# Another order of work in the single-head stage, in normalised products and around head 11 of a transformer kernel

## The reference, cut to what matters

```python
q = x @ w_q.T; k = ctx @ w_k.T; v = ctx @ w_v.T
x = x + alpha * (softmax(q @ k.T / sqrt(512)) @ v) @ w_o.T      # single-head stage
for i in (1, 2):                                                # two layers
    h = layer_norm(x) * scale_i + offset_i
    qh, kh, vh = heads(h @ wq + bq), heads(ctx @ wk + bk), heads(ctx @ wv + bv)
    kh, vh = append(kh, bias_k), append(vh, bias_v)             # one more key and value
    x = x + (softmax(qh @ kh.T / sqrt(128)) @ vh) @ wo + bo
h = layer_norm(x) * scale + offset
x = x + gelu(h @ w_fc1 + b_fc1) @ w_fc2 + b_fc2
```

## Time and profile before

| | us |
|---|---|
| median of 3 runs | 1877.48 |
| their range | 1876.43 to 1881.72 |
| the profiled execution, its own time | 1882.33 |
| its span (first to last instruction) | 1880.5 |
| PE busy | 1811.3 (96%) |
| DVE busy | 1131.0 (60%) |
| ACT busy | 805.8 (43%) |
| POOL busy | 767.4 (41%) |

### The profile page before, as it was taken

The page is one execution under the profiler, slowest core; times in us unless marked ns, Lnnn a source line. Parts: engine busy times, 40 slices in busy tenths (PEclk is TensorE's granted clock), DMA queues, the critical chain, the costliest instruction groups (busy, mean ns, idle before and its releaser), DMA issues.

```text
span 1880.5 us, 30389 instructions
## 1 busy us (share of the span) xinstructions
PE 1811.3 (96%) x11396; PEld 1769.5 (94%) x11396; DVE 1131.0 (60%) x2524; ACT 805.8 (43%) x1868; POOL 767.4 (41%) x634
## 2 busy tenths in 40 slices
PE   8778999999999999999999999999999999999999
PEld 4768999999999999999998999999999999999999
DVE  3556665566666655565578655556556556555565
ACT  3333443434434434444375533444435344434354
POOL 2466135253153342441368434244144242352244
PEclk9988999999999999999999999999999999999999
DMA  8743012121021121120372211112022011120122
GB/s 248 210 145 88 24 46 58 34 62 39 11 60 57 34 57 29 52 57 18 104 207 93 58 35 57 29 47 61 18 57 58 25 56 40 46 57 29 45 97 85
DMA packets 73589, 123.79 MB, mean 66 GB/s; under 512 B 13888, under 2 KB 25536, under 8 KB 73444
## 3 DMA queue, kind: packets, MB, share of 16 engines
q1 hardware_dynamic: 71140, 117.64, 21.6%
q10 hardware_dynamic: 2304, 4.20, 0.7%
HBM read 119.20 MB, written 2.61 MB: 65 GB/s over the span
## 4 chain that ended last, share of the span: by engine, by line
PE 88%; DVE 5%; POOL 3%; ACT 2%; issue 1%; DMA 1%; SPq 0%; DVEq 0%; ACTq 0%; POOLq 0%
PE psum L565 27%; PE psum L566 27%; PE psum L567 27%; PE psum L810 4%; PE psum L589 2%; POOL ctx_rows_lo L464 1%; PE psum L776 1%; DMA ctx_rows_in<-ctx_dram 1%; POOL w_lo L541 1%; POOL kw L484 1%; PE psum L688 1%; ACT sq L1040 1%; POOL w_lo L546 0%; DVE cen L1411 0%; DVE a_lo L1261 0%
## 5 line engine op out<-in xcount | busy, mean ns | idle before, releaser
L453 POOL TENSOR_TENSOR wbuf_hi<-stage,zero_col 128x512 fp32r<-128x512 f32 x256 | 266.7, 1042 | 934.7 <-PE psum L776 480.3
L500 POOL TENSOR_TENSOR wbuf_lo<-stage,wbuf_hi 128x512 fp32r<-128x512 f32 x256 | 329.4, 1287 | 20.1
L567 PE MATMUL psum<-pT_hi,ctx_rows_lo 121*128 121x250 f32 (+3 forms) x1152 | 332.2, 288 | 0.0
L565 PE MATMUL psum<-pT_hi,ctx_rows_hi 121*128 121x250 f32 (+3 forms) x1152 | 331.5, 288 | 0.0
L566 PE MATMUL psum<-pT_lo,ctx_rows_hi 121*128 121x250 f32 (+3 forms) x1152 | 331.0, 287 | 0.0
L565 PE MATMUL psum<-ctxT_hi,a_hi 128*125 128x362 f32 (+1 forms) x832 | 280.3, 337 | 3.5 <-DVE a_lo L1261 3.5
L567 PE MATMUL psum<-ctxT_hi,a_lo 128*125 128x362 f32 (+1 forms) x832 | 273.2, 328 | 0.0
L566 PE MATMUL psum<-ctxT_lo,a_hi 128*125 128x362 f32 (+1 forms) x832 | 272.6, 328 | 0.0
L1252 DVE TENSOR_TENSOR a_lo<-psum,a_hi 128x500 fp32r<-128x500 f32 (+2 forms) x288 | 146.2, 526 | 208.3 <-ACT a_hi L929 207.5
L565 PE MATMUL psum<-a_hi,wbuf_hi 128*128 128x400 f32 x720 | 253.8, 352 | 4.5 <-issue 4.5
L566 PE MATMUL psum<-a_lo,wbuf_hi 128*128 128x400 f32 x720 | 247.8, 344 | 0.0
(11 more groups left out here) (170 smaller groups left out, 3592.4 us busy)
## 6 DMA issues: line engine op xcount, KB each, us to landing
stage<-head_w_dram SPq DMA_DIRECT2D x256, 256.0 KB, 2.6
mlp_stage<-mlp_w_dram SPq DMA_DIRECT2D x32, 512.0 KB, 3.8
ctx_rows_in<-ctx_dram SPq DMA_DIRECT2D x12, 726.0 KB
ctxT_in<-ctxT_dram SPq DMA_DIRECT2D x12, 724.0 KB, 12.2
key_stage<-head_w_dram SPq DMA_DIRECT2D x32, 256.0 KB, 4.7
l0w<-l_w_dram ACTq DMA_DIRECT2D x16, 256.0 KB, 13.5
kb<-diff_scratch SPq DMA_DIRECT2D x32, 64.0 KB, 3.9
out_dram<-y_out SPq DMA_DIRECT2D x8, 200.0 KB, 2.3
```

The costliest lines, as they stand in the source:

```text
L453: return nc.gpsimd.tensor_tensor(out, in_, zero_col[0:in_.shape[0], :].broadcast_to(tuple(in_.shape)), ALU.add)
L500: nc.gpsimd.tensor_tensor(lo, held, hi.bitcast(F32), ALU.subtract).then_inc(stage_free, 1)
L565: pe.matmul(out, a_h, x_hi, start=start, stop=False)
L567: return pe.matmul(out, a_l, x_hi, start=False, stop=stop)
```

## The change

- SP waits for the first pair of `l0w` before it issues anything. The small tensors come ahead of the context rows of batch 0, and `diff` is written out between the loads; the loads of turn 1 are placed by what they wait for, and four key loads instead of seven stand behind the output transfer.
- PE makes the query weights alone, then the value weights in four groups: one before `queries0`, one after it, two after the first scores.
- ACT and DVE take the splits in another order; the split of `x1` moves from g = 0 to g = 1, the splits of the second turn's context to other places, and the 32 key sums are dealt out differently. POOL's products too.
- `prob0` and `w0` move to the space of the weight buffers, for which POOL gets one wait more.
- `product_of_norm` takes the place of `product` with `normed`: eight matmuls with the high part first, each chunk waiting for `n_hi`, then the four with the low part.
- `v11` moves from "last turn" to the end of (5, 0, "b"), `o11` from "last attend" to "last turn". The place "last attend" goes.

```diff
-    (5, 0, "b"): "v10 q15 o10 k15",
-    "last turn": "v11",
-    "last attend": "o11",
+    (5, 0, "b"): "v10 q15 o10 k15 v11",
+    "last turn": "o11",
...
+            sp.wait_ge(l0w_ld[0], 32)
-            load_ctx_rows(0, 0)
...
-            for b in range(1, NB):
-                load_ctx_columns(0, b)
-                load_ctx_rows(0, b)
+            load_ctx_rows(0, 0)
+            load_ctx_columns(0, 1)
             sp.wait_ge(diff_s, 1)
             sp.dma_start(diff_d, diff[:, 0, :]).then_inc(diff_out, 16)
+            load_ctx_rows(0, 1)
+            load_ctx_columns(0, 2)
+            load_ctx_rows(0, 2)
+            load_ctx_columns(0, 3)
+            load_ctx_rows(0, 3)
...
-            for i in range(4):
-                load_key_weights(i)
...
+            some_key_weights(4)
+            for b in range(2):
+                sp.wait_ge(ls_mm, b + 1)
+                load_ctx_columns(1, b)
             sp.wait_ge(lw_mm, 8)
             sp.dma_start(x1[:, :, :], xT_d[1]).then_inc(x_ld[1], 16)
             sp.dma_start(alpha_col[:, :], alpha_d.partition_broadcast(P)).then_inc(alpha_ld, 16)
             sp.dma_start(mlp_b[:, :], mlp_b_d).then_inc(mlp_b_ld, 16)
-            for i in range(4, 8):
-                load_key_weights(i)
-            for b in range(NB):
-                sp.wait_ge(ls_mm, b + 1)
-                load_ctx_columns(1, b)
-                sp.wait_ge(lu_mm, b + 1)
-                load_ctx_rows(1, b)
-                load_key_weights(8 + 2 * b)
-                load_key_weights(9 + 2 * b)
-            for i in range(16, 25):
-                load_key_weights(i)
+            some_key_weights(2)
+            sp.wait_ge(ls_mm, 3)
+            load_ctx_columns(1, 2)
+            sp.wait_ge(lu_mm, 1)
+            load_ctx_rows(1, 0)
+            some_key_weights(2)
+            sp.wait_ge(ls_mm, 4)
+            load_ctx_columns(1, 3)
+            sp.wait_ge(lu_mm, 2)
+            load_ctx_rows(1, 1)
+            some_key_weights(3)
+            sp.wait_ge(lu_mm, 3)
+            load_ctx_rows(1, 2)
+            some_key_weights(1)
+            sp.wait_ge(lu_mm, 4)
+            load_ctx_rows(1, 3)
+            some_key_weights(16)
             sp.wait_ge(lr_done, 2 * DC)
             sp.dma_start(out_d[1], xT[:, :, :]).then_inc(landed, 16)
-            for i in range(25, LAYERS * H):
-                load_key_weights(i)
+            some_key_weights(4)
...
             ctx_rows_lo(1, 0)
             some_key_weights(4)
             ctx_rows_lo(1, 1)
-            some_key_weights(3)
+            some_key_weights(2)
             ctx_rows_lo(1, 2)
-            some_key_weights(3)
+            some_key_weights(2)
-            some_key_weights(LAYERS * H - 18)
+            some_key_weights(LAYERS * H - 16)
...
+                        if ph == 0 and i == WBUFS - 2:
+                            pool.wait_ge(lp_mm, TURNS * NB)
...
+            def product_of_norm(out, a_h, a_l, j, n):
 
                 for c in range(DC):
-                    before(c)
+                    pe.wait_ge(n_hi, n_chunks(j, n, c))
+                    pe.matmul(out, a_h(c), h_hi[:, c, piece(n)], start=(c == 0), stop=False)
+                    pe.matmul(out, a_l(c), h_hi[:, c, piece(n)], start=False, stop=False)
+                for c in range(DC):
+                    pe.wait_ge(n_lo, n_chunks(j, n, c))
+                    mm = pe.matmul(out, a_h(c), h_lo[:, c, piece(n)], start=False, stop=(c == DC - 1))
+                return mm
...
-                for j in range(2):
+                for c in range(DC):
+                    pe.wait_ge(l0w_ld[c], 32)
+                    for g in range(DC):
+                        mm = pe.matmul(bank[g], chunk(l0w[0][:, c, :], g), l0w[1][:, c, :], start=(c == 0), stop=(c == DC - 1))
+                        if c == DC - 1:
+                            mm.then_inc(lw_mm, 1)
+
+                def value_weights(g):
                     for c in range(DC):
-                        pe.wait_ge(l0w_ld[j * DC + c], 32)
-                        for g in range(DC):
-                            mm = pe.matmul(bank[j * DC + g], chunk(l0w[2 * j][:, c, :], g), l0w[2 * j + 1][:, c, :],
-                                           start=(c == 0), stop=(c == DC - 1))
-                            if c == DC - 1:
-                                mm.then_inc(lw_mm, 1)
+                        pe.wait_ge(l0w_ld[DC + c], 32)
+                        mm = pe.matmul(bank[DC + g], chunk(l0w[2][:, c, :], g), l0w[3][:, c, :], start=(c == 0),
+                                       stop=(c == DC - 1))
+                    mm.then_inc(lw_mm, 1)
...
+                    if g < 2:
+                        pe.wait_ge(lw_lo, DC + g + 1)
...
                     pe.wait_ge(ls_norm, g + 1)
+                    if g == 0:
+                        pe.wait_ge(lw_lo, DC + 3)
...
+                    if g == 0:
+                        pe.wait_ge(lw_lo, 2 * DC)
...
+                value_weights(0)
                 queries0()
-                pe.wait_ge(lw_lo, 8)
+                value_weights(1)
                 pe.wait_ge(lq_lo, DC)
                 pe.wait_ge(const_ready, 3)
                 scores0(0)
                 scores0(1)
+                value_weights(2)
+                value_weights(3)
...
-                run_pieces("last attend")
...
+                for g in range(DC):
+                    weights_hi(0, g)
+                weights_hi(1, 0)
                 ctx_columns_hi(0, 0)
+                queries0_hi(0)
                 ctx_rows_hi(0, 0)
+                queries0_hi(1)
                 ctx_columns_hi(0, 1)
-                weights_hi(0)
+                queries0_hi(2)
                 ctx_rows_hi(0, 1)
+                queries0_hi(3)
                 ctx_columns_hi(0, 2)
-                weights_hi(1)
-                queries0_hi(0)
+                weights_hi(1, 1)
                 ctx_rows_hi(0, 2)
-                queries0_hi(1)
+                exp0(0)
                 ctx_columns_hi(0, 3)
-                queries0_hi(2)
-                queries0_hi(3)
+                exp0(1)
+                weights_hi(1, 2)
                 ctx_rows_hi(0, 3)
-                exp0(0)
-                exp0(1)
+                weights_hi(1, 3)
                 for g in range(TURNS * NB):
                     turn, b = divmod(g, NB)
                     probs0_hi(g)
-                    if g == 0:
-                        act.wait_ge(x_ld[1], 16)
-                        copy(x1_hi[:, :, :], x1[:, :, :]).then_inc(x_hi_s, 1)
                     if b < 2:
                         exp0(g + 2)
...
                     if b > 0:
                         turned_hi(g - 1)
                     rows_of(g)
+                    if g == 1:
+                        act.wait_ge(x_ld[1], 16)
+                        copy(x1_hi[:, :, :], x1[:, :, :]).then_inc(x_hi_s, 1)
+                        ctx_columns_hi(1, 0)
                     if g == 2:
-                        ctx_columns_hi(1, 0)
+                        ctx_columns_hi(1, 1)
                         ctx_rows_hi(1, 0)
                     if g == 3:
+                        ctx_columns_hi(1, 2)
                         queries1_hi(2)
                         turned_hi(g)
-                        ctx_columns_hi(1, 1)
+                        ctx_rows_hi(1, 1)
                         queries1_hi(3)
-                        ctx_rows_hi(1, 1)
                         exp0(4)
-                        ctx_columns_hi(1, 2)
                         exp0(5)
+                    if g == 4:
                         ctx_columns_hi(1, 3)
                         ctx_rows_hi(1, 2)
-                    if g == 4:
+                    if g == 5:
                         ctx_rows_hi(1, 3)
...
+                nc.vector.memset(prob0[:, :, 0:1], 0.0)
+                for g in range(DC):
+                    weights_lo(0, g)
+                weights_lo(1, 0)
                 ctx_columns_lo(0, 0)
-                ctx_columns_lo(0, 1)
-                weights_lo(0)
-                ctx_columns_lo(0, 2)
-                weights_lo(1)
                 queries0_lo(0)
                 queries0_lo(1)
-                ctx_columns_lo(0, 3)
+                ctx_columns_lo(0, 1)
                 queries0_lo(2)
                 queries0_lo(3)
-                dve.wait_ge(lw_mm, 8)
-                nc.vector.memset(prob0[:, :, 0:1], 0.0)
+                ctx_columns_lo(0, 2)
+                weights_lo(1, 1)
                 maxima0(0)
                 normalise0(0)
                 maxima0(1)
+                ctx_columns_lo(0, 3)
+                weights_lo(1, 2)
+                weights_lo(1, 3)
                 for g in range(TURNS * NB):
                     turn, b = divmod(g, NB)
                     if b < 2:
                         normalise0(g + 1)
...
-                    if g == 0:
-                        dve.wait_ge(x_hi_s, 2)
```

(17 more changed lines are left out.)

45 lines of the change are left out of this document (22 added, 23 removed).

## The result

| | before | after |
|---|---|---|
| median of 20 runs each, side by side, us | 1878.32 | 1881.61 |
| their range | 1874.02 to 1881.72 | 1876.71 to 1890.81 |
| profiled execution, its own time | 1882.33 | 1890.81 |
| its span | 1880.5 | 1889.0 |
| centring begins (end of the single-head stage) | 151.62 | 160.00 |

Ratio 1.0023, 95% interval 1.0013 to 1.0033: the change makes the kernel 2 to 6 us slower. 1867.5 was forecast, with a range of 1859 to 1876.

What follows compares the result with a forecast made beforehand. PE was taken as the bound (88% of the last-ending chain), so only its idle or slow time could be won. Stage -6.0, norm products -3.0 and layers -1.0 sum to -10.0: 1877.48 to 1867.5 us, range 1859 to 1876.

Steps and rivals of the forecast that it cites:

- lead of 14 us at `attend0(4)`: Single-head stage: `attend0(4)` starts at about 92 against 106.55, putting the change 14 us ahead.
- chains of turn 1: Second turn: DVE's key sums wait for GpSimd products queued behind context-row splits; together they give back 12.7 of 14 us.
- Start: Up to the first turn of probabilities: first matmul at 5.0, that turn at 48.4 against 53.76, gain 5.4 us.
- none is first in line at PE then: Start of the kernel: SP's later loads may start dry for about a microsecond, but PE waits for none of them.
- Turn 0: First turn: `x1` gives back some 4 us, but two holes close; `attend0(4)` at about 92, 14 us ahead.
- 3.7 us for `x1`: First turn: `queries1(0)` waits some 3.7 us because splitting `x1` moves behind `rows_of(1)` on ScalarE and DVE.
- Turn 1: From `attend0(4)` to `attend0(6)`: steps of 13.3 and 15.9 us, before 8.5 and 8.0; `attend0(6)` at about 121.
- rival (d): Single-head stage: late second-turn transfers leave `attend0(4)` only 3 us or less earlier; slower, 1880 to 1883; chance 0.06.
- Tail: End of the single-head stage: keys, not PE, end it; centring at 144.3 to 147.0, stage gain taken as 6.0 us.
- Norm products: Six norms: high matmuls first, low four last; gain 1.2 to 9 us, taken as 3.0.
- Pieces: Layer ends, `v11` and `o11` moved: gaps of 0.88 and 1.12 replaced by about 2.0; 1.0 us gained over four layers.
- rival (c): Layer ends: the single 2.0 us gap lets the clock fall each time, 4 x 3 = 12 back, 1879.5; chance 0.07.

Runs made afterwards that it cites:

- second execution of after: The changed kernel, unchanged, run and profiled again beside the others: 1882.14 us, ratio 1.0017 to the kernel before; centring begins at 155.53.
- ACT-order run: After with GpSimd's key weights four and four, and ScalarE's and VectorE's context splits behind ready work before the batch loop: 1876.02 us, ratio 0.9996 to before.
- chains cut: After with GpSimd's order alone changed: four key weights ahead of each of two `ctx_rows_lo`, instead of two: 1876.24 us, ratio 0.9997 to before.
- additions apart: DVE's four head-11 output additions split two and two around the last `probs_lo`: after with four-and-four key weights, 1868.91 us (0.9955); before with moved pieces, 1871.03 (0.9970).
- both latencies covered: `o10` ahead of the last turn, `o11` behind: after with four-and-four key weights, 1869.44 us (0.9963); before with norm products, 1869.56 (0.9965).

## Why the prediction was wrong

The step that failed is the lead of 14 us at `attend0(4)`, which was to pay for the chains of turn 1; it was 2 and 5 us. Its first part is "Start", where the landing of SP's loads was taken as cheap. The whole miss is 14.1 us: 11 in the stage (-6.0 forecast, about +5 measured), 2 in the layers (-4.0 forecast, -2.1 measured), and the rest is within the intervals. In the second execution of after, whose time is the more typical, the stage is 9.9 us behind the forecast's 145.6: 4.4 from the start, 5.0 more by `attend0(4)`, 0.1 in the two steps and 0.4 in the tail. About 2 more come from the kernel before, whose profiled execution ended the stage 2.0 us later than the mean of seven.

- **Start, -5.4.** First matmul forecast at 5.0, measured 4.46 and 4.63. The sentence "none is first in line at PE then" was wrong. With SP held, its loads land later (rows (0,1) by 3.8 us, columns (0,2) by 5.2), and as ACT's queue has splits of them ahead of `q_hi(3)` and `weights_hi(1, 1)`, PE pays: 53.23, 0.5 before the old kernel. The ACT-order run takes these splits out of the way and gets 48.30 for 48.4. That lead alone did not change the time (1876.02 against 1876.24 with the chains cut), so it is where the working first went wrong, but no run shows that it costs the kernel much. The Trainium skill, DMA: Bandwidth & Descriptors, section Queues, rings and completion order, lets the engines alternate between queues with work. This case's rows agree: the first pair lands at the early end when SP is silent, and SP's transfers pay what `l0w` gains.
- **Turn 0, 14 us ahead at `attend0(4)`.** It was 2 in the profiled execution, 5 in the second, 8 with the chains cut (98.10). The 3.7 us for `x1` came as forecast (3.69). Missing are the 4.4 to 4.8 from the start, and waits of sums for late key products ahead of `attend0(3)` (2.66 us of idle PE in the second execution) and of the turn of batch 4 (1.93), a kind of chain that the forecast priced only in turn 1. In the profiled execution the slow scaling ahead of `attend0(0)` comes on top. The forecast let context columns meet GpSimd's splits, not this scaling.
- **Turn 1, steps of 13.3 and 15.9.** Measured 13.6 and 15.7, and 13.4 and 15.7. This step was right, releaser and all, and cutting the chains gave back 3.8 to 4.9 of the about 5 us that the stage lost. The 12.7 it takes is no longer covered by a lead, which is rival (d)'s rule: it loses wherever `attend0(4)` starts less than 9 us earlier. Its 1880 to 1883 holds the measured 1881.61. It was given 0.06, with another reason for the small lead (late loads of turn 1; in fact late loads of turn 0 and late key products).
- **Tail.** From `attend0(6)` to centring 26.1 us in after, 25.0 in its second execution, forecast 24.6 (121 to about 145.6). Eight sums remained, as said. The terms that are written out add up to 143.9 to 146.5, not 144.3 to 147.0.
- **Norm products, -3.0.** Measured -3.6, with an interval of -1.9 to -5.1. At the second layer's norm PE starts 1.72 us behind the square sums in place of 2.56, and from those sums to the third product it takes 8.79 in place of 9.40. The size was right; the six terms were not measured one by one.
- **Pieces, -1.0.** The gap was sized (2.0 forecast, 1.67 measured), its clock was not: the forecast left falls of the clock to rival (c). In ten executions with this gap, the clock fell behind 27 of 40; 1.7 us each, so (c)'s 3 us a fall was too much, and nothing was too little. That the clock fell after two of the four holes of the earlier trace rows was a misreading: three of them are followed by a matmul of 0.75 us. Expected value by rows: -1.3 + 4 x 27/40 x 1.7 = +3.3. The ratios give +0.2 alone and +1.5 on top of the norm products. The moved pieces with the additions apart also come out about 2 us better than their rows (-5.6 for 4 x (1.02 - 2.00) = -3.9); no run shows why.

So the miss is a trade priced on one side (SP's hold), a lead that was therefore too small for chains that were sized right, and a clock fall taken as improbable. What stays open: no experiment controlled when the key loads land, which decides whether DVE's scaling or GpSimd's split starts first and how long sums wait; and none kept the chains of the change while it restored the lead.

The best versions, not to be told apart, are the kernel before with norm products, moved pieces and the additions apart (0.9947), and after with cut chains and the additions apart (0.9955). So the new single-head stage, even mended, won nothing that these runs measure.

## What to carry to other kernels

Holding back one DMA queue to let another through is a trade: find the first instruction, in any in-order queue, that waits for the held transfers, and see what ready work stands behind it. A split, sum or copy that waits for a foreign product should stand behind everything that is ready; price each such place, not only the worst. And look at the granted clock behind each gap: shortening a gap from 1.67 to 1.02 us was worth two to three times the 2.6 us of idle time here (5.8 to 7.9 us by the ratios of three pairs of kernels).

## What the runs showed of the hardware

- Behind a PE gap of 1.67 or 1.68 us the clock fell to half in 27 of 40 cases and cost 1.7 us each; behind gaps of 1.02 or 1.12 us in the same stretch of six kernels, in 0 of 24, and behind the 1.40 us of the two kernels with both latencies covered, in 0 of 8.
- DVE's scaling of 100 x 361 probabilities took 0.41 us, and 2.76 or 3.38 where GpSimd's subtraction of context rows had started before it; it ended 0.2 us after the subtraction did. The Trainium skill, SBUF — State Buffer, section SBUF: two separate sides, calls the shared port pair an exclusive lock; these rows agree, and show it at up to eight times the duration, where the forecast reckoned with instructions that double.
- SP's queue alone moved 212 to 223 GB/s, both queues together up to 401, at nearly the same busy share of the engines.
